# Causal attention: one mask matmul in front of a bank's scores, in place of one behind each score

## The chip, the cores and the metric

The kernel runs on one core of a Trainium2 chip. The metric is the device time of one execution in microseconds; the time before is a median of three runs.

## The reference

Four layers run one after another over x of 8 sequences x 512 rows x 256: causal attention, attention with four experts behind it ("ffn"), attention with relative positions over 256 steps, and the ffn layer again. Only the first is touched:

```python
attn = jnp.einsum('bhqd,bhkd->bhqk', q, k) * scale          # 16 heads of 16
causal = jnp.tril(jnp.ones((t, t), dtype=bool))
attn = jnp.where(causal, attn, -jnp.inf)
attn = _custom_softmax(attn)    # clip to +-100, max, exp, sum + 1e-6, + 1e-8, normalise again
out = jnp.einsum('bhqk,bhkd->bhqd', attn, v)
```

## The kernel before

`attention` walks over sequences n (0 to 7 are the causal layer, 8 to 15 the first ffn layer; both run in one stream). A sequence has 4 groups g of 4 heads, and a group 4 slots kt, one for each block of 128 keys. In a slot the engines run hand-written programs, in step by semaphores.

TensorE makes scores twice. `score` (L474) makes them with queries on partitions, two groups ahead, into a ring of three banks of PSUM, `sc`; VectorE reduces each unit to maxima (`row_max`, L769). `score_t` (L495) makes them with keys on partitions and the maximum already subtracted, into a ring of two banks, `sct`; ScalarE takes exponentials of each unit (`exp`, L690), VectorE clips them (`clip`, L798), and `pv` (L526, L534) multiplies by v. The stacked operands are bf16 in 96 or 99 rows, q and k being split in three parts each.

In the causal layer a unit holds as many heads as fit a bank of 512 columns. For `score` with qt = 0 that is four heads of 128 columns, with qt = 1 two of 256, with qt = 2 and 3 one of 384 or 512. For `score_t` it is the other way round: kt = 3 four heads, kt = 2 two, kt = 1 and 0 one. So each group has 11 units in either direction. Behind each head's score a second matmul adds the mask of the diagonal block, 128 columns: identity times `mask_qk` (L477) or `mask_kq` (L498), which hold 0 or -1e30. Only the last matmul of a unit tells the reader (`sc_ps`, `t_ps`), and a unit's first waits until its bank is free (`max_done`, `exp_done`).

`floor_row` (L509) is a matmul of 3 rows and 512 columns into the `sct` ring, whose exponential gives the lower clip (L697). Between units a slot fits in a "light" use of bank gen1 (transposes L404, L438, L446, L457) and, at its end, half of a "heavy" use of bank gen0 (L413, L421, L430: f32 projections of the neighbouring sequences). A heavy use stands behind the last unit of the slot: at kt = 0 and 1 that is a `score_t` unit, at kt = 2 and 3 a floor row. `heavy_at` names one for slots 0 to 7 and 12 to 15, and for 8 to 11 that of the sequence before. In the first sequence slots 0 to 3 and 8 to 11 have none.

Of the kernel before, what the change touches and what calls it, by code (L numbers as in the profile page):

```python
# [12 lines left out]
P = 128  # L13
NB, T, D = 8, 512, 256
# [35 lines left out]
def attention(nc, M, R, S, C, A, layers, first, end, units):  # L50
# [10 lines left out]
    def causal(n):  # L61
        return layers[n // NB].causal
# [16 lines left out]
    last = end - 1  # L79
# [25 lines left out]
    def score_heads(n, qt, i):  # L105

        if causal(n) and qt == 0:
            return (0, 1, 2, 3) if i == 0 else ()
        if causal(n) and qt == 1:
            return (i, i + 1) if i % 2 == 0 else ()  # L110
        return (i,)

    def max_unit(n, g, qt, i):

        at = (0, 1 + i // 2, 3 + i, 7 + i)[qt] if causal(n) else 4 * qt + i
        return sum(NG * MAX_UNITS[causal(m)] for m in range(n)) + MAX_UNITS[causal(n)] * g + at

    def exp_heads(n, kt, i):

        if causal(n) and kt == 3:  # L120
            return (0, 1, 2, 3) if i == 0 else ()
        if causal(n) and kt == 2:
            return (i, i + 1) if i % 2 == 0 else ()
        return (i,)

    def floors_at(n, g, kt):

        fn, fg = group(n, g + 1)
        if not (exists(fn) and causal(fn)):
            return {}  # L130
        return {i: (fn, fg, h) for i, h in {2: ((1, 0), (3, 1)), 3: ((1, 2), (3, 3))}.get(kt, ())}
# [10 lines left out]
    for n in range(first, end):  # L142
        for g in range(NG):
            for kt in range(KT):
                for i in range(4):
                    if exp_heads(n, kt, i):
                        number((n, g, kt, i))
                    if i in floors_at(n, g, kt):
                        fn, fg, h = floors_at(n, g, kt)[i]
                        number((fn, fg, "floor", h))  # L150

    def exp_unit(n, g, kt, i):
        return unit_no[(n, g, kt, i)]
# [72 lines left out]
    with nc.Block(no_gpsimd_drain=True) as block:  # L226
# [161 lines left out]
        def _(pe):  # L388
# [71 lines left out]
            def score(n, g, qt, i):  # L460

                heads = score_heads(n, qt, i)
                if not heads:
                    return
                if qt == 0 and i == 0:
                    pe.wait_ge(S.stack_loaded[g], 64 * (n + 1))
                u = max_unit(n, g, qt, i)
                if u >= 3:
                    pe.wait_ge(S.max_done, u - 2)
                bank = M.sc[u % 3]  # L470
                cols = P * (qt + 1) if causal(n) else T
                for at, h in enumerate(heads):
                    o = at * cols
                    last = nc.tensor.matmul(bank[:, o:o + cols], M.stack_q[0:96, g, h, qt * P:qt * P + P], M.stack_k[0:96, g, h, 0:cols],  # L474
                                            start=True, stop=True)
                    if causal(n):
                        last = nc.tensor.matmul(bank[:, o + qt * P:o + qt * P + P], C.ident_bf[:, :], C.mask_qk[:, :],  # L477
                                                start=False, stop=True, skip_group_check=True)
                last.then_inc(S.sc_ps, 1)

            def score_t(n, g, kt, i):

                heads = exp_heads(n, kt, i)
                if not heads:
                    return
                if kt == 0 and i == 0 and not causal(n):
                    pe.wait_ge(S.max_rows[g], 16 * (n + 1))
                u = exp_unit(n, g, kt, i)
                if u >= 2:
                    pe.wait_ge(S.exp_done, u - 1)  # L490
                bank = M.sct[u % 2]
                q0 = kt * P if causal(n) else 0
                for at, h in enumerate(heads):
                    o = at * (T - q0)
                    last = nc.tensor.matmul(bank[:, o:o + T - q0], M.stack_k[0:99, g, h, kt * P:kt * P + P], M.stack_q[0:99, g, h, q0:T],  # L495
                                            start=True, stop=True)
                    if causal(n):
                        last = nc.tensor.matmul(bank[:, o:o + P], C.ident_bf[:, :], C.mask_kq[:, :],  # L498
                                                start=False, stop=True, skip_group_check=True)
                last.then_inc(S.t_ps, 1)  # L500

            def floor_row(n, g, i):
# [42 lines left out]
            def slot(n, g, kt):  # L545
                s = KT * g + kt
                tn, tg = group(n, g + 2)
                floors = floors_at(n, g, kt)
                light, heavy = light_at(n, s), heavy_at(n, s)
                for i in range(4):  # L550
                    score_t(n, g, kt, i)
                    if exists(tn):
                        score(tn, tg, kt, i)
                    if i in floors:
                        floor_row(*floors[i])
                    if i == (2 if kt == KT - 1 else 0) and light:
                        use_bank(light)
                    if i == (2 if causal(n) else 1):
                        pv_before(n, g, kt)
                if heavy:  # L560
                    use_bank(heavy, halves=(s % 2,))
# [3 lines left out]
            for qt in range(KT):  # L565
                for i in range(4):
                    score(first, 0, qt, i)
                use_bank(opening[8 + qt])
            for qt in range(KT):
                for i in range(4):  # L570
                    score(first, 1, qt, i)
                if qt < 3:
                    use_bank(opening[12 + qt])
# [2020 lines left out]
```

## Time and profile before

| | |
|---|---|
| median of three runs | 2650.02 us (2644.34 to 2658.11) |
| the profiled execution, device time | 2654.06 us |
| its span, first to last instruction | 2652.3 us |
| instructions | 46652 |
| TensorE's mean granted clock | 0.971 of full |
| TensorE, VectorE, ScalarE, POOL busy | 93%, 69%, 54%, 50% of the span |

An engine's busy time is the union of its instructions. Matmul rows overlap: a row's duration holds the stream of its columns and the tail of the pipeline, so the pitch between starts, not the duration, is what a matmul costs in a row of them. "PEld" is the loading of weights, which can run under the matmul before it.

### The profile page before, as it was taken

How to read it: one execution, taken by the hardware profiler on the slowest of the kernel's cores; microseconds unless marked ns; L12 is line 12 of the kernel's file. 1: busy time of each engine (PE TensorE's matmuls, PEld its weight loads, DVE VectorE, ACT ScalarE, POOL GpSimd, SP SyncE). 2: the span in 40 equal slices, each digit the busy share in tenths (PEclk: the TensorE clock that was granted, in tenths of full speed). 3: DMA queues.
4: the chain of work that ended last, by engine and by line, in shares of the span. 5: the costliest groups of instructions: out<-in, count | busy, mean ns of one | idle time of the engine just before them, and what ended most of it. 6: DMA issues, size and time to landing. Idle time of an engine off the chain costs nothing. (4 is left out here: it accounts for less than half of the span.)

```text
span 2652.3 us, 46652 instructions
## 1 busy us (share of the span) xinstructions
PE 2465.1 (93%) x15144; PEld 1430.2 (54%) x15144; DVE 1835.1 (69%) x3682; ACT 1438.0 (54%) x2991; POOL 1332.1 (50%) x1349
## 2 busy tenths in 40 slices
PE   6999999999999999989996899976999999989998
PEld 3555555554444444368886466652344444349897
DVE  5988999898788887843333457666778888844333
ACT  3666666666777777643332222113777777753332
POOL 5455666553345554246555466644235554445555
PEclk9999999999999999999998799988999999999999
DMA  5333333343434444145554000004434444335554
GB/s 161 94 109 97 109 108 101 106 117 101 121 113 126 126 130 120 53 150 193 195 177 155 22 1 17 17 24 133 120 109 131 129 129 121 94 113 168 195 195 137
DMA packets 249650, 305.92 MB, mean 115 GB/s; under 512 B 27746, under 2 KB 224577, under 8 KB 249412
## 3 DMA queue, kind: packets, MB, share of 16 engines
q1 hardware_dynamic: 237876, 275.37, 34.8%
q0 software_dynamic: 10176, 26.27, 2.8%
q8 instruction: 125, 2.05, 0.3%
q10 hardware_dynamic: 1360, 1.31, 0.2%
q14 instruction: 113, 0.93, 0.1%
HBM read 210.32 MB, written 92.84 MB: 114 GB/s over the span
## 5 line engine op out<-in xcount | busy, mean ns | idle before, releaser
L769 DVE TENSOR_REDUCE neg_max_af<-sc_af 128x1 f32<-128x512 f32 (+3 forms) x864 | 551.1, 663 | 109.5 <-PE sc_af L474 84.5
L690 ACT ACTIVATE prob_af<-sct_af 128x512 f32<-128x512 f32 (+1 forms) x864 | 484.5, 582 | 249.1 <-PE sct_af L495 137.4
L769 DVE TENSOR_REDUCE neg_max_f<-sc_f 128x1 f32<-128x512 f32 x512 | 334.0, 685 | 92.1 <-PE sc_f L474 90.1
L690 ACT ACTIVATE prob_f<-sct_f 128x512 f32<-128x512 f32 x512 | 291.0, 598 | 134.8 <-PE sct_f L495 133.0
L474 PE MATMUL sc_af<-stack_k_af,stack_q_af 96*128 96x512 bf16 (+3 forms) x1024 | 332.2, 345 | 19.3 <-DVE neg_max_af L769 13.4
L495 PE MATMUL sct_af<-stack_q_af,stack_k_af 99*128 99x512 bf16 (+3 forms) x1024 | 331.3, 346 | 5.2 <-ACT prob_af L690 4.4
L1598 PE MATMUL y_ps_e<-w_r,hT_e 128*128 x1120 | 258.5, 384 | 7.5 <-issue 5.6
L798 DVE SCALAR_TENSOR_TENSOR prob_af<-prob_af,w_r 128x512 f32<-128x512 f32 (+2 forms) x224 | 231.5, 1042 | 25.9 <-ACT prob_af L690 25.7
L526 PE MATMUL out_af<-prob_af,v_aug_af 128*32 128x512 f32 (+3 forms) x2048 | 232.3, 525 | 6.8 <-DVE prob_af L798 5.9
L1598 PEld LDWEIGHTS y_ps_e<-w_r,hT_e 128*128 128x128 f32 x1120 | 209.4, 192 | 38.4 <-issue 11.9
L495 PEld LDWEIGHTS sct_af<-stack_q_af,stack_k_af 99*128 99x128 bf16 x1024 | 100.1, 98 | 228.5 <-ACT prob_af L690 147.6
L1783 DVE TENSOR_TENSOR y_e<-y_ps_e,b_e 128x256 f32<-128x256 f32 x70 | 29.7, 425 | 279.4 <-PE y_ps_e L1598 276.7
L1611 PE MATMUL hT_ps_e<-xT_e,w_r 128*128 128x128 f32 x1856 | 219.7, 277 | 3.2 <-DMA w_r<-in_f_W_dram 2.0
L1611 PEld LDWEIGHTS hT_ps_e<-xT_e,w_r 128*128 128x128 f32 x1856 | 218.0, 194 | 7.2 <-DMA w_r<-in_f_W_dram 3.1
L474 PE MATMUL sc_f<-stack_k_f,stack_q_f 96*128 96x512 bf16 x512 | 195.4, 387 | 20.4 <-DVE neg_max_f L769 13.3
L1668 ACT ACTIVATE xT_e<-xT_ps_e 128x256 f32<-128x256 f32 x70 | 26.9, 385 | 332.4 <-PE xT_ps_e L1589 332.4
L495 PE MATMUL sct_f<-stack_q_f,stack_k_f 99*128 99x512 bf16 x512 | 195.3, 384 | 4.5 <-ACT prob_f L690 3.3
L474 PEld LDWEIGHTS sc_af<-stack_k_af,stack_q_af 96*128 96x128 bf16 x1024 | 102.1, 100 | 127.6 <-DVE neg_max_af L769 54.0
L1679 ACT ACTIVATE hT_e<-hT_ps_e,b_r 128x128 f32<-128x128 f32 x560 | 152.8, 383 | 32.1 <-issue 25.7
L1050 POOL TENSOR_TENSOR parts_af<-qkf_af,parts_af 128x512 bf16<-128x512 f32 x62 | 76.6, 1236 | 127.7 <-ACT parts_af L668 127.6
L526 PE MATMUL out_f<-prob_f,v_aug_f 128*32 128x512 f32 x1024 | 137.0, 607 | 0.8 <-ACT prob_f L690 0.7
L495 PEld LDWEIGHTS sct_f<-stack_q_f,stack_k_f 99*128 99x128 bf16 x512 | 49.6, 98 | 159.0 <-ACT prob_f L690 120.1
(373 smaller groups left out, 4744.7 us busy)
## 6 DMA issues: line engine op xcount, KB each, us to landing
w_r<-in_f_W_dram SPq DMA_DIRECT2D x66, 1024.0 KB, 5.0
stack_k_af<-k_parts_d SPq DMA_DIRECT2D x64, 384.0 KB, 4.2
k_parts_d<-parts_af SPq DMA_DIRECT2D x187, 128.0 KB
q_parts_d<-parts_af SPq DMA_DIRECT2D x96, 128.0 KB
stack_q_af<-q_parts_d SPq DMA_DIRECT2D x64, 192.0 KB, 3.0
stack_k_f<-k_parts_d SPq DMA_DIRECT2D x32, 384.0 KB, 4.3
w_next<-in_f_W_dram SPq DMA_DIRECT2D x12, 1024.0 KB, 4.9
k_parts_d<-parts_f SPq DMA_DIRECT2D x91, 128.0 KB
```

Source lines behind the costliest of these rows:

```text
L474: last = nc.tensor.matmul(bank[:, o:o + cols], M.stack_q[0:96, g, h, qt * P:qt * P + P], M.stack_k[0:96, g, h, 0:cols], start=True, stop=True)
L495: last = nc.tensor.matmul(bank[:, o:o + T - q0], M.stack_k[0:99, g, h, kt * P:kt * P + P], M.stack_q[0:99, g, h, q0:T], start=True, stop=True)
L526: last = nc.tensor.matmul(bank[32 * i:32 * i + 32, q0:T], M.v_aug[:, kt, 4 * g + i, :], M.prob[:, kt % 2, i, 0:T - q0], start=(kt == 0), s ...
L690: nc.scalar.activation(dst, src.rearrange("p (h q) -> p h q", h=len(heads)), ACT.Exp).then_inc(S.exp_done, 1)
L769: nc.vector.tensor_reduce(M.neg_max[:, qt, heads[0]:heads[-1] + 1], src, AX.X, ALU.max, negate=True).then_inc(S.max_done, 1)
L798: nc.vector.scalar_tensor_tensor(out=p, in0=p, scalar=1.0, in1=M.floor[:, g % 2, hs, kt * P:T], op0=ALU.min, op1=ALU.max).then_inc(S.clip_ ...
L1050: nc.gpsimd.tensor_tensor(M.parts[:, j, 1, :], full, top, ALU.subtract).then_inc(S.split_step, 1)
L1598: last = nc.tensor.matmul(y_ps[:, 0:D], hT[s % 2][:, c, :], w2[:, c, e, :], start=(c == 0), stop=(c == FC - 1))
L1611: last = nc.tensor.matmul(hT_ps[2 * (s % 2) + f][:, q * P:q * P + P], w1[n % NW][:, c, cols], xT[:, c, :], start=(c == 0), stop=(c == DC - 1))
L1668: nc.scalar.activation(xT[:, :, :], xT_ps[:, 0:D].rearrange("p (c t) -> p c t", c=DC), ACT.Copy).then_inc(xT_ready, 1)
L1679: last = nc.scalar.activation(hT[s % 2][:, 4 * f + q, :], hT_ps[2 * (s % 2) + f][:, q * P:q * P + P], ACT.Relu, bias=b1[:, e, 4 * f + q:4 ...
L1783: nc.vector.tensor_tensor(y[i][:, :], y_ps[:, 0:D], b2[:, e, :], ALU.add).then_inc(y_ready, 1)
```

## The change

In the causal layer `score` and `score_t` now begin a unit with one matmul that writes the masks of all heads of the bank: the output is a view of heads x 128 columns, the moving operand is the mask repeated with a step of 0, and it starts the bank. The scores follow without a start, so they add where the mask has written and overwrite elsewhere. The unit's last matmul, which tells the reader, is now a score. Layers that aren't causal get the instructions they had.

```diff
--- before.py
+++ after.py
@@ -469,13 +469,15 @@
                     pe.wait_ge(S.max_done, u - 2)
                 bank = M.sc[u % 3]
                 cols = P * (qt + 1) if causal(n) else T
+                masked = causal(n)
+                if masked:
+                    diagonal = bank[:, 0:len(heads) * cols].rearrange("p (h k) -> p h k", h=len(heads))[:, :, qt * P:qt * P + P]
+                    nc.tensor.matmul(diagonal, C.ident_bf[:, :], C.mask_qk[:, :].unsqueeze(1).to_broadcast([P, len(heads), P]),
+                                     start=True, stop=True)
                 for at, h in enumerate(heads):
                     o = at * cols
                     last = nc.tensor.matmul(bank[:, o:o + cols], M.stack_q[0:96, g, h, qt * P:qt * P + P], M.stack_k[0:96, g, h, 0:cols],
-                                            start=True, stop=True)
-                    if causal(n):
-                        last = nc.tensor.matmul(bank[:, o + qt * P:o + qt * P + P], C.ident_bf[:, :], C.mask_qk[:, :],
-                                                start=False, stop=True, skip_group_check=True)
+                                            start=not masked, stop=True, skip_group_check=masked)
                 last.then_inc(S.sc_ps, 1)
 
             def score_t(n, g, kt, i):
@@ -490,13 +492,15 @@
                     pe.wait_ge(S.exp_done, u - 1)
                 bank = M.sct[u % 2]
                 q0 = kt * P if causal(n) else 0
+                masked = causal(n)
+                if masked:
+                    diagonal = bank[:, 0:len(heads) * (T - q0)].rearrange("p (h q) -> p h q", h=len(heads))[:, :, 0:P]
+                    nc.tensor.matmul(diagonal, C.ident_bf[:, :], C.mask_kq[:, :].unsqueeze(1).to_broadcast([P, len(heads), P]),
+                                     start=True, stop=True)
                 for at, h in enumerate(heads):
                     o = at * (T - q0)
                     last = nc.tensor.matmul(bank[:, o:o + T - q0], M.stack_k[0:99, g, h, kt * P:kt * P + P], M.stack_q[0:99, g, h, q0:T],
-                                            start=True, stop=True)
-                    if causal(n):
-                        last = nc.tensor.matmul(bank[:, o:o + P], C.ident_bf[:, :], C.mask_kq[:, :],
-                                                start=False, stop=True, skip_group_check=True)
+                                            start=not masked, stop=True, skip_group_check=masked)
                 last.then_inc(S.t_ps, 1)
 
             def floor_row(n, g, i):
```

The first place is on TensorE, in the slot s = 4 of a sequence (kt = 0), where a score unit of four heads stands between two score_t units of one head. In the changed kernel L475 and L498 are the masks, L479 and L502 the scores.

```order
+L475 MATMUL sc_af<-mask_qk,ident_bf 128x512
+L479 MATMUL sc_af<-stack_k_af,stack_q_af 128x128 x4
 L404 MATMUL gen_af<-ident,w_2_r 128x128 x4
-L495 MATMUL sct_af<-stack_q_af,stack_k_af 128x512
-L498 MATMUL sct_af<-mask_kq,ident_bf 128x128
-L495 MATMUL sct_af<-stack_q_af,stack_k_af 128x512
-L498 MATMUL sct_af<-mask_kq,ident_bf 128x128
```

The four masks of 128 columns have become one of 512 ahead of four scores; the pairs of score and mask that the removed rows show are turned round (below).

The second place is the end of that slot on TensorE: the last score_t unit, the heavy use L430, and the first units of the next slot.

```order
+L498 MATMUL sct_af<-mask_kq,ident_bf 128x128
+L502 MATMUL sct_af<-stack_q_af,stack_k_af 128x512
 L430 MATMUL gen_af<-wa_o,attT_af 128x256 x2
-L495 MATMUL sct_af<-stack_q_af,stack_k_af 128x384
-L498 MATMUL sct_af<-mask_kq,ident_bf 128x128
-L474 MATMUL sc_af<-stack_k_af,stack_q_af 128x256
-L477 MATMUL sc_af<-mask_qk,ident_bf 128x128
-L474 MATMUL sc_af<-stack_k_af,stack_q_af 128x256
-L477 MATMUL sc_af<-mask_qk,ident_bf 128x128
+L498 MATMUL sct_af<-mask_kq,ident_bf 128x128
+L502 MATMUL sct_af<-stack_q_af,stack_k_af 128x384
+L475 MATMUL sc_af<-mask_qk,ident_bf 128x2x128
```

L430 stood behind a mask of 128 columns and now stands behind a score of 512; the two-head unit's masks have become one of 2 x 128 columns. The other engines' programs keep their instructions and their order.

## Rows read from the trace of the kernel before

**Rows 1.** The page, busy us of each engine, share, instructions
```profile
PE 2465.1 (93%) x15144; PEld 1430.2 (54%) x15144; DVE 1835.1 (69%) x3682; ACT 1438.0 (54%) x2991; POOL 1332.1 (50%) x1349
```

**Rows 2.** Windows: length, busy us of PE, PEld, DVE, ACT, POOL, then granted clock
```profile
60.00:120.00 60.00, 57.65 (x498) 29.95 (x498) 54.65 (x106) 40.77 (x77) 20.92 (x22) 0.94 0.39 106
120.00:600.00 480.00, 468.31 (x3987) 254.67 (x3987) 438.26 (x827) 317.75 (x588) 284.78 (x255) 0.98 0.37 105
600.00:620.00 20.00, 18.94 (x146) 9.29 (x144) 19.76 (x37) 11.52 (x21) 2.07 (x3) 1.00 0.24 68
```

**Rows 3.** Waits from 120 to 600 us: us in total, times, longest
```profile
ACT prob_af L690 <- PE sct_af L498: 90.4, 134, 1.8
...
PEld sc_af L474 <- DVE neg_max_af L769: 28.6, 49, 0.8
...
PEld sct_af L495 <- ACT prob_af L690: 24.6, 52, 0.8
DVE prob_af L798 <- ACT prob_af L690: 23.4, 42, 1.4
...
DVE neg_max_af L769 <- PE sc_af L477: 7.2, 22, 0.4
...
DVE neg_max_af L769 <- PE sc_af L474: 1.2, 1, 1.2
```

**Rows 4.** Timeline, a score_t unit of four heads: start, us, engine, line
```profile
300.58 0.22 PE L495 MATMUL sct_af<-stack_q_af,stack_k_af 99*128 99x128 bf16 x1
...
300.99 0.22 PE L498 MATMUL sct_af<-mask_kq,ident_bf 128*128 128x128 bf16 x1
```

**Rows 5.** Timeline, a score unit of one head, and the next
```profile
301.05 0.38 PE L474 MATMUL sc_af<-stack_k_af,stack_q_af 96*128 96x512 bf16 x1
...
301.27 0.22 PE L477 MATMUL sc_af<-mask_qk,ident_bf 128*128 128x128 bf16 x1
```

**Rows 6.** Timeline, a score unit of two heads
```profile
310.05 0.27 PE L474 MATMUL sc_af<-stack_k_af,stack_q_af 96*128 96x256 bf16 x1
...
310.16 0.22 PE L477 MATMUL sc_af<-mask_qk,ident_bf 128*128 128x128 bf16 x1
...
310.22 0.27 PE L474 MATMUL sc_af<-stack_k_af,stack_q_af 96*128 96x256 bf16 x1
```

**Rows 7.** Timeline, a score_t unit behind a wait
```profile
73.49 0.10 PEld L495 LDWEIGHTS sct_af<-stack_q_af,stack_k_af 99*128 99x128 bf16 x1 [0.23 <-issue]
73.50 0.23 PE L495 MATMUL sct_af<-stack_q_af,stack_k_af 99*128 99x128 bf16 x1
...
73.56 0.22 PE L498 MATMUL sct_af<-mask_kq,ident_bf 128*128 128x128 bf16 x1
```

**Rows 8.** Timeline, a mask with f32 weights behind it
```profile
308.85 0.22 PE L498 MATMUL sct_af<-mask_kq,ident_bf 128*128 128x128 bf16 x1
308.85 0.30 PEld L430 LDWEIGHTS gen_af<-wa_o,attT_af 128*128 128x128 f32 x2
308.91 0.43 PE L430 MATMUL gen_af<-wa_o,attT_af 128*128 128x256 f32 x1
```

**Rows 9.** Line L430 from 120 to 600 us: ns min/median/max
```profile
L430 PE MATMUL gen_af<-wa_o,attT_af x104: 377/379/483, 166.0 to 597.9; 128*128 128x256 f32 x104
```

**Rows 10.** Timeline, four f32 matmuls of 256 columns
```profile
308.91 1.08 PE L430 MATMUL gen_af<-wa_o,attT_af 128*128 128x256 f32 x4
```

**Rows 11.** Windows of TensorE's clock at its lower level, and of two lulls
```profile
138.90:142.30 3.40, 2.40 (x18) 0.59 (x15) 3.40 (x7) 1.08 (x2) 3.15 (x4) 1.00 0.54 191
142.40:145.70 3.30, 3.30 (x14) 1.81 (x15) 2.72 (x9) 1.52 (x3) 0.00 (x0) 0.50 0.46 114
...
569.10:572.40 3.30, 3.30 (x15) 1.86 (x14) 2.88 (x9) 1.65 (x3) 0.00 (x0) 0.50 0.47 112
352.00:357.00 5.00, 4.00 (x29) 1.68 (x28) 4.90 (x12) 1.76 (x4) 4.39 (x4) 1.00 0.54 192
```

## The prediction

> **What bounds the kernel now.** I began with the page's busy shares [rows 1]: TensorE is busy for 93% of the span, VectorE for 69%. A busy matmul row holds its pipeline's tail too, so 93% doesn't yet say that TensorE is the bound. The windows by stage [rows 2] come next. The causal layer's steady part is the stretch from 60 to 620 us, at 0.98 of TensorE's full clock in its middle; almost nothing that the diff touches runs elsewhere. In its middle 480 us TensorE shows 468.3 us and VectorE 438.3 us, ScalarE 317.8 and POOL 284.8: two engines are near their limit. The waits of that stretch [rows 3] say who is late for whom. VectorE waits 23.4 us for exponentials of ScalarE and 7.2 + 1.2 us for scores: 31.8 us in 480. ScalarE waits for a score_t unit that ends in a mask 90.4 us (134 times). TensorE's weight loads wait 28.6 us for a maximum to free a score bank and 24.6 us for an exponential to free a score_t bank. So it is a ring of three engines: TensorE fills a bank, ScalarE or VectorE empties it, and VectorE, with 438.3 busy and 31.8 waiting, is nearest to being the bound. A microsecond saved on TensorE is worth at most a microsecond, and nothing where a bank was the late thing.
>
> **What the change removes.** Each group of four heads has, in either direction, one unit of four heads (128 columns each), two units of two heads (256 each) and eight units of one head. There are 8 sequences x 4 groups x 2 directions = 64 such sets. Before, a set holds 16 mask matmuls of 128 columns = 2048 columns; after, one of 512, two of 256 and eight of 128 = 2048 columns. **No column is saved**; 5 matmuls and 5 weight loads per set are, 320 of each.
>
> What one is worth is read from its pitch. In the four-head unit eight matmuls of 128 columns start from 300.58 to 300.99 [rows 4]: 0.41 / 7 = 0.058 us each, loads included, so loads are hidden. The durations 0.22 and 0.38 for 128 and 512 columns [rows 4, 5] give 0.16 / 384 = 0.417 ns a column, 53 ns per 128, so about 5 ns of each matmul is fixed. A two-head unit goes 0.11, 0.06 [rows 6] and agrees. Saved: 320 x 5 ns = **1.6 us** of TensorE. The Trainium skill, "TensorE: Matmul & The Clock Gate", section "Wait — 56ns, not 53.3ns?", gives 2.5 ns as the fixed part; by it the sum would have 0.8 us here. The trace's pitch is the longer one.
>
> **What the change moves.** The mask goes from the end of a unit to its front. Four consequences.
>
> (a) The wait for a bank now stands ahead of the mask's weight load, not ahead of the score's. Queued behind it are the same matmuls, so nobody waits longer. Would a short first matmul expose the next load? At 73.49 a unit starts behind such a wait with a 128-column matmul at 73.50, and the next starts at 73.56 [rows 7]: 0.06, the usual pitch. The bounds are nothing, and one exposed stream of 0.05 us at each of the 101 loads that ended a wait in the middle 480 us (49 + 52), 5 us there and 6 in the stage. I take 0, since the row is the very case.
>
> (b) The last matmul of a unit, which releases ScalarE or VectorE, is now the score. For one head its end is the same sum: 0.22 + 0.06 before, 0.06 + 0.22 after. Cost 0.
>
> (c) A score now adds to the mask's columns, and the distance between two writes of one column stays 128 columns or more, as from 301.05 to 301.27 before [rows 5], where the mask followed without a gap. Cost 0.
>
> (d) What follows a unit follows a long matmul, not one of 58 ns. That matters for f32 weights. At 308.85 the mask starts and with it the load of L430's f32 weights; the matmul starts at 308.91 and takes 0.43 [rows 8], while the median of L430 is 379 ns [rows 9]. So 0.43 - 0.38 = 0.05 us of the load is exposed. After the change a score of 384 or 512 columns (at least 0.16 us) covers it. This place (a "heavy" bank use right behind the last score_t unit, with no wait that drains the queue between) comes at slots with kt 0 or 1, 8 per sequence, less 4 in the first: 60 x 0.05 = **3.0 us**. At kt 2 and 3 a floor row of 512 columns stands between already, and nothing changes.
>
> Sum: 1.6 + 3.0 = 4.6 us of TensorE's time, 0.17% of the run. VectorE, ScalarE, POOL and both DMA queues issue what they did, in their order. How much arrives? If TensorE were the bound everywhere, 4.6; if VectorE were, none. With VectorE waiting 31.8 us in the ring and TensorE's loads 53.2 us for banks, I take somewhat under half: **2 us**. The profiled execution took 2654.06 us (span 2652.3), 4.0 above the median of the three runs, 2650.02; so I expect about 2652.1 for a like execution and **2648.0** for the median.
>
> **A cost the trace doesn't show.** The masks of two heads are written as two runs of 128 columns with a gap of 128, and the moving mask is read again and again by a step of 0. No matmul of before writes such a pattern. The Trainium skill, "PSUM — Partial Sum Buffer", section "Specifications (TRN2)", says that any non-contiguous access pattern slows matmuls significantly, which speaks against this change. From rows: the lower end is no cost, a bf16 row of 256 columns at 0.11 [rows 6]. The upper end is what f32 takes for as many columns: four matmuls of 256 fill 1.08 us, the last one's 0.38 among it, so the pitch is 0.70 / 3 = 0.23 [rows 9, 10], and 0.46 for 512. That is 128 x (0.23 - 0.11) + 64 x (0.46 - 0.22) = 15.4 + 15.4 = 31 us. I take 0, because each run is 128 columns long and the nearest row is that of the same type.
>
> **The rivals.**
> 1. *Nothing arrives.* VectorE's 438.3 of 480 us sets the pace and the 4.6 us become longer waits of weight loads. Time 2650.0.
> 2. *Slower: the pattern.* The strided or repeated mask runs slower. The saving is eaten when the 192 wide masks take over 4.6 / 192 = 24 ns more each; at the upper end 31 - 4.6 = 26.4 us are lost and the time is 2676. Against it: each run is long. At half of the upper end 2661.
> 3. *Faster: the clock.* TensorE's clock stood at its lower level, 1.2 GHz (granted 0.50), in five stretches of some 3.3 us between 120 and 600 us (the first and the last stand in [rows 11]), the first after a lull at 138.9 to 142.3, where TensorE was busy 2.40 of 3.40 us; near 352 us a similar lull (4.00 of 5.00) had none. Each costs half its length, 1.7 us. If the shift removes all five and all of the 4.6 us arrives: 8.5 + 4.6 = 13.1, time 2637. The same thing can add the missing ones, +3 us or so.
> 4. *The change doesn't do what it says.* If scores beside the diagonal added to a bank's old values, results would change, but no engine's row would: all counts of instructions are fixed. Time as forecast.
>
> **How the numbers follow.** The forecast has a chance of 0.58, rival 1 0.22, rival 2 0.08, rival 3 0.10, rival 4 0.02. A measurement of this kernel can tell about 0.5%, 13.3 us, from no change: under 2636.8 or over 2663.3. Rival 3, whose end lies at the line, gives 0.06 beyond it and 0.04 within; rival 2 gives 0.06 beyond and 0.02 within. So 0.06 faster, 0.88 the same, 0.06 slower. The range: low end, all 4.6 us and three clock stretches gone, 2650 - 4.6 - 5.1 = 2640; high end, no gain, two stretches more and a quarter of the pattern's upper price less the saving (7.7 - 4.6 = 3.1), 2650 + 3.4 + 3.1 = 2656.5, taken as 2657.
>
> **What would show it.** In the profile after, masks on TensorE number 704, in forms of 128, 256 and 512 columns. A four-head unit starts its scores 0.22 us behind the mask and a two-head one 0.11; 0.4 or more there means rival 2. L430 behind a score takes 379 ns, not 0.43 us. ScalarE's wait for the last matmul of a score_t unit and VectorE's 31.8 us fall by a few us together. If instead the loads' waits for banks (53.2 us) grow by what was saved, rival 1 is right. The prediction is wrong if the time leaves 2640 to 2657 with clock and pitches as before.

## The result and the profile after

The changed kernel takes **2639.38 us** (median of five, 2636.45 to 2640.8) against 2650.5 us, the median of the kernel before with two more runs; the ratio is 0.9953 (95% interval 0.9933 to 0.9974). Timed again beside other kernels (12 runs) it took 2639.61 us, ratio 0.9957 (0.9940 to 0.9974). So 11 us came where 2 were forecast, and the time lies 0.6 us under the range's low end of 2640.

The page of the kernel after, its busy times [rows 1 before]:

```profile
span 2637.6 us, 46012 instructions
...
PE 2443.5 (93%) x14824; PEld 1406.5 (53%) x14824; DVE 1837.7 (70%) x3682; ACT 1437.0 (54%) x2991; POOL 1334.0 (51%) x1349
```

TensorE lost exactly 320 matmuls and 320 loads. VectorE, ScalarE and POOL have their counts and, within 3 us, their busy time. The windows of the causal layer [rows 2]:

```profile
60.00:120.00 60.00, 57.61 (x463) 28.74 (x463) 54.94 (x107) 40.47 (x77) 20.59 (x22) 0.94 0.40 111
120.00:600.00 480.00, 465.65 (x3784) 244.68 (x3785) 446.31 (x844) 322.32 (x596) 287.95 (x257) 1.00 0.37 106
```

In the same 480 us VectorE does 446.3 us of work, not 438.3, and TensorE's clock is at 1.00, not 0.98. The waits of that stretch [rows 3]:

```profile
ACT prob_af L694 <- PE sct_af L502: 84.2, 132, 1.9
...
PEld sc_af L475 <- DVE neg_max_af L773: 33.4, 60, 0.8
...
PEld sct_af L498 <- ACT prob_af L694: 25.8, 56, 0.8
...
DVE prob_af L802 <- ACT prob_af L694: 18.4, 38, 1.4
...
DVE neg_max_af L773 <- PE sc_af L479: 5.4, 14, 1.2
```

VectorE waits 18.4 + 5.4 = 23.8 us, not 31.8, ScalarE 84.2, not 90.4, and the loads wait 33.4 + 25.8 = 59.2 us for banks, not 53.2. The PE timeline of a four-head unit with its neighbours, and of L430 behind a score [rows 4, 8]:

```profile
299.06 0.38 PE L502 MATMUL sct_af<-stack_q_af,stack_k_af 99*128 99x512 bf16 x1
299.28 0.38 PE L475 MATMUL sc_af<-mask_qk,ident_bf 128*128 128x512 bf16 x1
299.50 0.39 PE L479 MATMUL sc_af<-stack_k_af,stack_q_af 96*128 96x128 bf16 x4
```

```profile
305.13 0.27 PE L475 MATMUL sc_af<-mask_qk,ident_bf 128*128 128x256 bf16 x1
305.24 0.38 PE L479 MATMUL sc_af<-stack_k_af,stack_q_af 96*128 96x256 bf16 x2
...
306.78 1.03 PE L430 MATMUL gen_af<-wa_o,attT_af 128*128 128x256 f32 x4
```

The mask of four heads takes 0.22 us to the first score, the strided one of two heads 0.11. Four scores of 128 columns fill 0.39 us: (0.39 - 0.22) / 3 = 0.057 or a little less each. L430's four take 1.03 us, not 1.08 [rows 10]: the exposed 0.05 us is gone.

L413, another f32 projection, stood behind a mask in the slots kt 0 and 1 as well. Its ns (min, median, max) before and after, from 60 to 620 us; the median falls by 54 ns:

```profile
L413 PE MATMUL gen_af<-xnT_af,wa_qkv x96: 592/646/1183, 111.4 to 498.3; 128*128 128x512 f32 x96
```

```profile
L413 PE MATMUL gen_af<-xnT_af,wa_qkv x96: 590/592/1222, 110.4 to 491.3; 128*128 128x512 f32 x96
```

**Where the time went.** Two words first. TensorE's stream is what its instructions need one behind the other, by their pitches. A fall is a stretch of some 3.4 us in which TensorE's granted clock is 0.50, that is 1.2 GHz; a sequence without one is called undisturbed. The last read of a sequence's output (ScalarE, `o_sb`, L676 before, L680 after) marks the pace. Before:

```profile
128.61 0.64 ACT L676 ACTIVATE o_sb_af<-out_af 128x512 f32<-128x512 f32 x1
200.09 0.64 ACT L676 ACTIVATE o_sb_af<-out_af 128x512 f32<-128x512 f32 x1
343.03 0.64 ACT L676 ACTIVATE o_sb_af<-out_af 128x512 f32<-128x512 f32 x1
413.35 0.64 ACT L676 ACTIVATE o_sb_af<-out_af 128x512 f32<-128x512 f32 x1
555.11 0.64 ACT L676 ACTIVATE o_sb_af<-out_af 128x512 f32<-128x512 f32 x1
```

After:

```profile
127.44 0.64 ACT L680 ACTIVATE o_sb_af<-out_af 128x512 f32<-128x512 f32 x1
197.16 0.64 ACT L680 ACTIVATE o_sb_af<-out_af 128x512 f32<-128x512 f32 x1
336.59 0.64 ACT L680 ACTIVATE o_sb_af<-out_af 128x512 f32<-128x512 f32 x1
407.49 0.64 ACT L680 ACTIVATE o_sb_af<-out_af 128x512 f32<-128x512 f32 x1
546.92 0.64 ACT L680 ACTIVATE o_sb_af<-out_af 128x512 f32<-128x512 f32 x1
```

In each fence the first two rows are one sequence apart, the next two another, and from the first to the last are six. Before, a sequence takes 71.48 us (first pair) where TensorE's clock fell in it and 70.32 (second pair) or 70.28 (the next) where it did not: a fall costs about 1.2 us. After, it takes 69.72 without and 70.90 with. Six take 426.5 us before and 419.5 after. An undisturbed sequence is thus 70.28 - 69.71 = 0.57 us shorter, 8 x 0.57 = 4.6 us in the layer: **the whole saving of the stream**. The other part is falls. Before, they stand in four of the six sequences, three of them in a row. Windows of the kernel before [rows 11], and the one fall in the six after:

```profile
142.50:145.70 3.20, 3.20 (x14) 1.71 (x14) 2.62 (x8) 1.42 (x3) 0.00 (x0) 0.50 0.47 114
214.20:217.40 3.20, 3.20 (x16) 1.92 (x15) 2.81 (x9) 1.53 (x3) 0.00 (x0) 0.50 0.54 113
285.80:289.00 3.20, 3.20 (x17) 2.16 (x16) 3.02 (x10) 1.40 (x3) 0.00 (x0) 0.50 0.21 70
```

```profile
350.10:353.30 3.20, 3.20 (x8) 1.20 (x8) 2.91 (x9) 1.02 (x2) 0.00 (x0) 0.50 0.44 121
```

The falls before stand 71.7 us apart, and a sequence with a fall in it is 71.5 us long. That near match became the theory of the pace, below. The whole of the layer ends 11 us earlier (the `o_sb` of the eighth sequence ends at 631.1 before, 620.1 after).

### The profile page after: what moved, and what is told of

Its sections match the earlier page's. It is cut to its first block and busy times, and to the rows that moved or that the text cites. A ratio compares the mean times of both kernels' runs of the same rounds, so it can differ in the third digit from the quotient of the medians.

```text
span 2637.6 us, 46012 instructions
## 1 busy us (share of the span) xinstructions
PE 2443.5 (93%) x14824; PEld 1406.5 (53%) x14824; DVE 1837.7 (70%) x3682; ACT 1437.0 (54%) x2991; POOL 1334.0 (51%) x1349
## 5 line engine op out<-in xcount | busy, mean ns | idle before, releaser
L479 PE MATMUL sc_af<-stack_k_af,stack_q_af 96*128 96x512 bf16 (+3 forms) x1024 | 319.7, 342 | 11.1 <-DVE neg_max_af L773 10.9
L502 PE MATMUL sct_af<-stack_q_af,stack_k_af 99*128 99x512 bf16 (+3 forms) x1024 | 319.7, 343 | 5.1 <-ACT prob_af L694 3.9
L479 PE MATMUL sc_f<-stack_k_f,stack_q_f 96*128 96x512 bf16 x512 | 195.7, 388 | 21.6 <-DVE neg_max_f L773 14.3
L502 PE MATMUL sct_f<-stack_q_f,stack_k_f 99*128 99x512 bf16 x512 | 195.6, 384 | 5.5 <-ACT prob_f L694 3.9
L502 PEld LDWEIGHTS sct_af<-stack_q_af,stack_k_af 99*128 99x128 bf16 x1024 | 97.5, 98 | 193.0 <-ACT prob_af L694 115.9
L1683 ACT ACTIVATE hT_e<-hT_ps_e,b_r 128x128 f32<-128x128 f32 x560 | 152.4, 382 | 32.5 <-issue 25.8
L479 PEld LDWEIGHTS sc_af<-stack_k_af,stack_q_af 96*128 96x128 bf16 x1024 | 98.8, 99 | 81.5 <-DVE neg_max_af L773 21.9
L502 PEld LDWEIGHTS sct_f<-stack_q_f,stack_k_f 99*128 99x128 bf16 x512 | 49.7, 98 | 160.0 <-ACT prob_f L694 119.7
```

Of the source, the lines that this page charges most:

```text
L1683: last = nc.scalar.activation(hT[s % 2][:, 4 * f + q, :], hT_ps[2 * (s % 2) + f][:, q * P:q * P + P], ACT.Relu, bias=b1[:, e, 4 * f + q:4 ...
```

## The experiments

Each kernel was timed beside the kernel before on the same chip, and profiled. The table reads three things from each profile by the `o_sb` rows and the granted clock: an undisturbed sequence, the falls of the clock in six sequences, and the time of the six. The kernel before and the changed one have several profiles; their falls and times stand in order (after, after_again, after_third, after_side). Not all kernels were timed on the same chip, so they are best compared by their ratios.

| kernel | median us | ratio (interval) | undisturbed, us | falls | six, us |
|---|---|---|---|---|---|
| before | 2648.6 to 2652.8 | 1 | 70.28 | 4, 4, 3 | 426.5, 426.5, 425.3 |
| after | 2639.4, 2639.6 | 0.9953, 0.9957 | 69.71 | 1, 2, 2, 1 | 419.5, 420.7, 422.6, 419.5 |
| order_only | 2640.28 | 0.9966 (0.9946 to 0.9986) | 69.89 | 0 | 419.4 |
| merge_only | 2641.63 | 0.9974 (0.9957 to 0.9991) | 70.07 | 1 | 421.6 |
| heavy_front | 2640.59 | 0.9970 (0.9955 to 0.9986) | 69.97 | 1 | 421.0 |
| after_mask_twice | 2653.32 | 1.0016 (0.9998 to 1.0035) | 71.45 | 0 | 428.8 |
| twice_score_t | 2652.18 | 1.0009 (0.9989 to 1.0028) | 70.88 | 2 | 428.4 |
| twice_score | 2649.05 | 0.9993 (0.9974 to 1.0012) | 71.17 | 1 | 428.3 |
| before_lull_filled | 2655.07 | 1.0012 (0.9994 to 1.0031) | 70.28 | 2 | 424.5 |
| after_lull_filled | 2648.17 | 0.9995 (0.9979 to 1.0011) | 69.72 | 2 | 422.6 |
| after_paced | 2644.54 | 0.9985 (0.9963 to 1.0007) | 70.01 | 0 | 420.1 |
| before_slowed | 2654.49 | 1.0017 (0.9997 to 1.0037) | 70.93 | 2 | 428.6 |
| after_at_70 | 2649.55 | 1.0011 (0.9990 to 1.0033) | 70.32 | 3 | 428.1 |
| floor_first | 2633.85, 2630.61 | 0.9945, 0.9926 (0.9906 to 0.9946) | 69.15 | 3, 3 | 415.4, 415.3 |

### The parts of the change alone

**order_only**: every mask in front of its own score, none merged; `score` gets the same edit.

```diff
+                    front = causal(n)
+                    if front:
+                        nc.tensor.matmul(bank[:, o:o + P], C.ident_bf[:, :], C.mask_kq[:, :],
+                                         start=True, stop=True)
                     last = nc.tensor.matmul(bank[:, o:o + T - q0], ...
-                                            start=True, stop=True)
-                    if causal(n):
+                                            start=not front, stop=True, skip_group_check=front)
+                    if causal(n) and not front:
...
```

> Every head's mask stands in front of its own score, none is merged: 1024 masks of 128 columns as before. Stream theory (what TensorE's stream is shortened by arrives in full; the exposed f32 loads go, 3.0 us, the 320 matmuls stay): 2650.5 - 3 = 2647.5, an undisturbed sequence of the causal layer 70.3 - 0.4 = 69.9 us. Rival, the buffers set the pace and the gain of the change came from the falls of TensorE's clock alone: sequences stay at 70.3 us, and the time follows how many falls of the clock stand in the stage (six before, one after, each worth 1.2 us of the sequence it falls in).

**merge_only**: the changed kernel, but one-head units keep the mask behind.

```diff
-                masked = causal(n)
+                masked = causal(n) and len(heads) > 1
...
+                    if causal(n) and not masked:
+                        last = nc.tensor.matmul(bank[:, o:o + P], C.ident_bf[:, :], C.mask_kq[:, :], ...
```

> Units of two and four heads get the one mask in front, units of one head keep theirs behind the score. Stream theory: the 320 matmuls go (1.6 us), the exposed f32 loads behind one-head units stay: 2649, sequence 70.1 us. If instead the merge carries the gain, the time is that of the change, near 2639 to 2641, sequence 69.7 us.

**heavy_front**: the first edit in `score_t` alone, for the units ahead of a heavy use.

```diff
-                    front = causal(n)
+                    front = causal(n) and kt < 2 and i == 3
```

> Only the last score_t unit of the slots with kt 0 and 1 has its mask in front, 64 units, 60 of them with a heavy bank use behind. Stream theory: the first matmul of L413, L421 and L430 there loses its 0.05 us, 60 x 0.05 = 3.0 us, all of it arrives, 2647.5, the same as order_only. If the order matters elsewhere too (at every unit), order_only is faster than this by more than 1 us a stage and this one stays near 2650.

Undisturbed sequences went from 70.28 to 69.89, 70.07 and 69.97: 0.39, 0.21 and 0.31 us, times eight 3.1, 1.7 and 2.5 us, where 3.0, 1.6 and 3.0 were expected. The first two add up to 0.60, near the whole change's 0.57. **The stream theory holds to a tenth of a microsecond a sequence, and so does the split.** Most of the gain of the order (0.31 of 0.39) lies in 64 units of 704. But all three kernels are 7 to 9 us faster by their ratios, some 5 us more than their stream, and all three profiles have no fall or one where the kernel before has three or four. A cause beside the stream was needed.

### Is all of TensorE's stream the bound?

**after_mask_twice** issues the mask of each one-head unit twice; **twice_score_t** and **twice_score** do so in one direction.

```diff
                     nc.tensor.matmul(diagonal, C.ident_bf[:, :], C.mask_kq[:, :]...
+                    if len(heads) == 1:
+                        nc.tensor.matmul(diagonal, C.ident_bf[:, :], C.mask_kq[:, :]...
```

> The changed kernel with the mask of each one-head unit issued twice: 512 more matmuls of 0.058 us, 29.7 us of TensorE's stream, 3.7 a sequence. Stream theory: all of it arrives, 2639.4 + 29.7 = 2669, an undisturbed sequence 69.7 + 3.7 = 73.4 us. If VectorE or the buffers set the pace and TensorE has room: under half, 2639 to 2654, a sequence under 71.5 us.

> The changed kernel with the mask of the one-head score_t units (slots kt 0 and 1) issued twice: 256 x 0.058 = 14.8 us of TensorE's stream, 1.86 a sequence. Doubling both directions cost 1.76 of 3.71 us a sequence. Theory of places: in the slots kt 0 and 1 TensorE is the bound and all of it arrives, undisturbed sequence 69.7 + 1.8 = 71.5 us, time 2639 + 14 = 2653. Rival, the same half everywhere: 70.6 us, 2646.

> The same for the one-head score units (slots kt 2 and 3), 14.8 us of stream too. Theory of places: these slots wait for VectorE's maxima, TensorE has room, and nothing or little arrives: sequence 69.7 to 69.9 us, 2640. Rival, half everywhere: 70.6 us, 2646.

The sequence grew by 1.74 us for 3.71 us of stream; in score_t alone by 1.17 of 1.86, in score alone by 1.46 of 1.86. So the theory of places is wrong (in the slots kt 2 and 3, where little or nothing was to arrive, 1.46 us did), and so is half everywhere: each half costs well over half by itself, both together under half. Additions find room that the removals did not need; how that room is shared between the slots stays open. The waits of after_mask_twice from 120 to 600 us show VectorE drawn in:

```profile
DVE prob_af L808 <- ACT prob_af L700: 21.2, 45, 1.4
DVE neg_max_af L779 <- PE sc_af L482: 17.9, 53, 1.2
```

VectorE waits 39.1 us, against 23.8 after the change.

### The falls of the clock

**before_lull_filled** and **after_lull_filled** issue the two floor rows of slot 3 twice.

```diff
+                if fill:
+                    nc.tensor.matmul(M.sct[u % 2][:, :], M.stack_k[96:99, g, i, 0:P], M.stack_q[96:99, g, i, :],
+                                     start=True, stop=True)
...
-                        floor_row(*floors[i])
+                        floor_row(*floors[i], fill=s == 3)
```

> The kernel before, with the two floor rows of slot 3 of each causal sequence issued twice (16 more matmuls of 512 columns, 3.5 us of TensorE's stream), where TensorE stood idle for VectorE and the clock fell just behind. Clock theory: the falls of slot 3 go, each was worth 1.2 us, and the added stream lies in the lull: 2650 - 5 to 2650 - 6, about 2644, with undisturbed sequences of 70.3 us. Rival (falls are chance): no fewer falls, and the time is 2650 or up to 3.5 us more.

> The same filling in the changed kernel, which had one such fall. Clock theory: no gain, 2639 to 2642; sequences 69.7 us if the lull hides the filling, up to 70.1 if it doesn't. Rival: the same as before_lull_filled less 11 us.

> The kernel before, profiled once more. If the falls of TensorE's clock in the causal layer belong to the kernel (a sequence of 71.5 us with a fall in it, 71.7 us from fall to fall), this profile has 4 or more of them between 130 and 620 us again. If they are chance, it has 0 to 2, as the profiles of the variants had, and the six sequences take 422 us in place of 426.5.

> The changed kernel, profiled once more: 0 to 1 falls between 130 and 620 us if they belong to the kernel, any number to 5 if they are chance. The undisturbed sequence is 69.7 us either way.

The second profiles speak against chance in the kernel before, which has four falls again, at 141.7, 213.4, 425.0 and 496.7 (and a fifth at 568.4). For the changed kernel the expectation was missed: from 130 to 620 us it has three falls (349.5, 421.2, 561.1) where 0 to 1 were expected, two of them in the six sequences. The filling of the kernel before is half a miss. Its profile has undisturbed sequences of 70.28, so the lull hid the added stream, and two falls, not four. Yet the timed median is 2655, not 2644, and the filled changed kernel's 2648.17 is some 9 us over the changed kernel's. The filling does not simply remove falls, and why its timed runs were slower than its profiled stage is not explained here.

**after_paced** and **before_slowed** change the length of a sequence by doubled masks in slots kt 0 and 1, ten a sequence in the changed kernel and twenty in the old one.

```diff
+                    if kt == 0 and i in (1, 2) or kt == 1 and i == 1 and g in (0, 2):
+                        nc.tensor.matmul(diagonal, C.ident_bf[:, :], C.mask_kq[:, :]...
```

```diff
+                        for _ in range(2 if kt == 0 or kt == 1 and i == 1 else 1):
                             last = nc.tensor.matmul(bank[:, o:o + P], C.ident_bf[:, :], C.mask_kq[:, :], ...
```

> The changed kernel with ten masks a sequence issued twice in slots kt 0 and 1 (0.58 us), so that an undisturbed sequence is 70.3 us again, as before the change. Theory of the pace: TensorE's clock fell four times in six sequences before because a sequence with a fall in it, 71.5 us, is as long as the distance from fall to fall, 71.7, so one fall brings the next; here 3 to 5 falls again and 2649. Rival, the falls hung on what stood in the lull: 0 to 2 falls and only the added stream, 2639.4 + 4.6 = 2644.

> The kernel before with twenty masks a sequence issued twice in slots kt 0 and 1, 1.17 us of stream, 9.3 us in all, so that an undisturbed sequence is 71.4 us, as it was with a fall. Theory of the pace: a fall now makes a sequence of 72.6, which no longer meets the next fall, 0 to 1 falls in six sequences, and the time rises by 9.3 - 5 = 4 to 2654. Rival: four falls stay, 2650 + 9 = 2659.

Both missed their lengths, since about half of an addition arrives: 70.01 in place of 70.3, and 70.93 in place of 71.4. At 70.01 there was no fall and the time was the rival's, 2644.54. Its profile ends the layer as early as the changed kernel's do (621.9 us, against 621.2 in the mean), so the 5 us between the medians are not explained. At 70.93 there were two falls, between the theory's 0 to 1 and the rival's four, and the time rose by 4 us as the theory had it, though 5.2 us of stream arrived. Neither kernel had the length that it was made for, so neither tells the theories apart. **after_at_70** doubles the masks that before_slowed did, in the changed kernel.

```diff
+                    if kt == 0 or kt == 1 and i == 1:
+                        nc.tensor.matmul(diagonal, C.ident_bf[:, :], C.mask_kq[:, :]...
```

> The changed kernel with the mask of five score_t units a group issued twice (20 a sequence, 1.17 us of stream; half of such additions arrived so far), so that an undisturbed sequence is 70.3 us, as before the change. Theory of the pace: 3 to 5 falls of the clock in six sequences again, time 2649. Rival, the falls belong to the old order of instructions: 0 to 2 falls, time 2639.4 + 5 = 2644.

> The kernel before, third profile. Falls that belong to the kernel: 3 to 5 in six sequences, 425 to 427.5 us. Chance: 0 to 2.

> The changed kernel, third profile: 0 to 2 falls in six sequences and 418.3 to 420.7 us if the low count belongs to it, 3 or more if it is chance.

It has the new order and the old length. Its `o_sb` rows and windows:

```profile
127.97 0.59 ACT L683 ACTIVATE o_sb_af<-out_af 128x512 f32<-128x512 f32 x1
198.29 0.59 ACT L683 ACTIVATE o_sb_af<-out_af 128x512 f32<-128x512 f32 x1
```

```profile
211.70:214.90 3.20, 3.20 (x7) 1.17 (x7) 3.03 (x10) 0.73 (x2) 0.13 (x1) 0.50 0.40 121
283.40:286.60 3.20, 3.20 (x7) 1.17 (x7) 3.03 (x10) 0.73 (x2) 0.12 (x1) 0.50 0.36 108
355.10:358.30 3.20, 3.20 (x7) 1.17 (x7) 3.03 (x10) 0.73 (x2) 0.12 (x1) 0.50 0.41 123
358.30:361.50 3.20, 3.20 (x23) 2.19 (x25) 1.29 (x4) 2.03 (x4) 0.00 (x0) 0.50 0.67 160
426.80:430.00 3.20, 2.70 (x16) 0.86 (x17) 3.20 (x6) 0.82 (x2) 2.04 (x3) 1.00 0.47 163
```

A sequence is 70.32 us, three falls stand in a row 71.7 us apart, as in the kernel before (its third profile has 212.6, 284.3 and 356.0), and the time is 2649.55 us. The third of them is twice as long as the others, as its two windows show. The median is 10 us over the changed kernel's (15 by the ratios), where 8 x 0.61 = 4.9 us of stream arrived, and the layer ends at 630.7 us in the profile, where it ended at 630.0 before the change and at 621.2 after it in the mean. The execution profiled took 2641.37 us all the same, at the low end of its kernel's: the layers behind were short in it.

All profiles together say more than this one. In the five whose undisturbed sequence is 70.28 to 70.33 us (the kernel before three times, before_lull_filled, after_at_70), 12 of the 16 falls in the six sequences were followed by another 71.7 us later. In those of another length, floor_first aside, it was 1 of 15. before_lull_filled fits in: its falls at 423.8 and 495.5 are a chain with a third at 567.2. In all of these kernels the falls in the six sequences begin 13.3 to 14.2 us behind the start of the `o_sb` row ahead of them.

**The falls go with the length of the sequence rather than with the order of the masks**: a fall comes at nearly the same place in a sequence, it stretches the sequence to 71.5 or 71.7 us, and that is nearly the distance at which the next fall then came. At 69.7 to 70.1 us the chain breaks after one or two. What begins a chain, and why some kernels have a single fall and others none, stays open. The third profile of the changed kernel has its two falls, as expected, but takes 422.6 us for the six, over the 420.7 expected, because one of the two is of double length. Its windows:

```profile
349.30:352.50 3.20, 3.20 (x6) 1.06 (x6) 3.01 (x10) 0.85 (x2) 0.10 (x1) 0.50 0.25 71
352.60:355.80 3.20, 3.20 (x29) 2.30 (x31) 1.62 (x3) 2.14 (x5) 0.00 (x0) 0.50 0.79 199
```

### The same mechanism where the change didn't reach

**floor_first**: in slots kt 2 and 3 the floor row of i = 3 goes ahead of the score unit, so that a heavy use follows a score, with no wait between.

```diff
                     score_t(n, g, kt, i)
+                    if i in floors and i == 3:
+                        floor_row(*floors[i])
                     if exists(tn):
                         score(tn, tg, kt, i)
-                    if i in floors:
+                    if i in floors and i != 3:
                         floor_row(*floors[i])
```

> The changed kernel with the floor row of i = 3 (slots kt 2 and 3) ahead of the score unit, not behind it, so that the heavy f32 matmuls there follow a score with no wait between: their first matmul falls from 697 to 592 ns (L413) or from 483 to 379 (L421, L430), 60 x 0.105 = 6.3 us of stream. Theory that a saving ahead of the projections arrives in full: 2639.4 - 6.3 = 2633, an undisturbed sequence 69.7 - 0.8 = 68.9. Rival, the score unit now waits behind the floor row's bank and VectorE gets its scores later: 69.7 or more, 2640 to 2645.

> The changed kernel beside floor_first. If the gain of the change is 4.6 us of stream and some 5 us of falls of the clock: 8 to 11 us under the kernel before. If the falls were luck of the first occasion, 4 to 6 us under.

> 0.55 us a sequence less than the changed kernel in its profile (69.15 against 69.7), 4.4 us in all: 4 to 6 us under after_side. Rival, the falls of the clock it had (three) take it back: 0 to 2 us under.

Beside the changed kernel on one chip it took 2630.61 us against 2639.61, 9 us less, and 0.9926 (0.9906 to 0.9946) of the kernel before: **it beats both**. The first time, on another chip, it took 2633.85 us, as expected, but its ratio was 0.9945, only just under the changed kernel's 0.9953 and 0.9957, so how much it gains on that one is less sure than that it does. Its `o_sb` rows in the second profile:

```profile
125.66 0.64 ACT L682 ACTIVATE o_sb_af<-out_af 128x512 f32<-128x512 f32 x1
194.81 0.64 ACT L682 ACTIVATE o_sb_af<-out_af 128x512 f32<-128x512 f32 x1
...
540.92 0.64 ACT L682 ACTIVATE o_sb_af<-out_af 128x512 f32<-128x512 f32 x1
```

L430 in the changed kernel, where 14 of its first matmuls follow a floor row and take 483 ns, and in floor_first (second profile), from 60 to 620 us:

```profile
L430 PE MATMUL gen_af<-wa_o,attT_af x112: 377/379/483, 163.4 to 597.8; 128*128 128x256 f32 x112
```

```profile
L430 PE MATMUL gen_af<-wa_o,attT_af x112: 377/378/382, 161.8 to 591.9; 128*128 128x256 f32 x112
```

The matmuls of 483 ns, 0.10 us longer than the median, are gone. A sequence is 69.15 us, 0.56 less where 0.8 was expected, and six take 415.3. It has three falls; two of them were followed by another after 68.3 us. They begin 12.4 to 13.9 us behind the `o_sb` row, near the place of the others, but each stretches its sequence by 0.15 us only; why so little stays open. 4.5 of the 9 us are stream; the expectation of 4 to 6 missed the rest.

## Why the prediction was wrong

**What was right.** The sizes in the stream: 1.6 us for the 320 matmuls (merge_only showed 1.7), 3.0 us for the f32 loads (order_only 3.1, heavy_front 2.5). The three terms put at nothing have little room to be more: order_only, which holds all three, saved 3.1 us where the f32 term alone is 3.0. Behind a wait the score follows its mask at the usual pitch, 306.55 and 306.62 in the changed kernel:

```profile
306.55 0.23 PE L498 MATMUL sct_af<-mask_kq,ident_bf 128*128 128x128 bf16 x1
306.62 0.33 PE L502 MATMUL sct_af<-stack_q_af,stack_k_af 99*128 99x384 bf16 x1
```

The unknown price was nothing too: the strided mask of two heads has a pitch of 0.11 us and the repeated one of four 0.22, those of plain rows. The Trainium skill, "PSUM — Partial Sum Buffer", says in "Specifications (TRN2)" that any non-contiguous pattern slows matmuls significantly; with runs of 128 columns the trace doesn't agree. Rival 2 fell.

**The step that failed** is "How much arrives?". I took 2 of 4.6 us because VectorE seemed nearest to the bound. All 4.6 arrived: 70.28 to 69.71 us a sequence. VectorE's 31.8 us of waits were the mark of TensorE's stream, and 8 of them went. Here a busy share of 91% in the second engine (438.3 of 480) was no sign that it takes a saving back. The sign I had named for rival 1 failed too: the loads' waits for banks did grow, by 6.0 us, beside the fall of the other engines' waits that I had named for the forecast. Both signs came at once, while the sequence got shorter, so the loads' waits can't tell the two apart. The "half" I expected holds for additions, which the runs put at 47 to 78%, not for this removal.

**The second error** was to treat the clock as luck that could only widen the range. Rival 3 named the mechanism and gave it 0.10, all or nothing. It was mostly systematic: the old length of a sequence invites a chain of falls (4, 4 and 3 in three profiles), the new one doesn't (1, 2, 2, 1). In the mean over the profiles of each kernel the six sequences take 5.5 us less (426.1 and 420.6): 3.4 of stream, and 2.1 for 2.2 falls fewer. With the opening and the eighth sequence, which hold the layer's other falls, it is 8.8 us by the end of the layer (630.0 and 621.2), 4.6 of it stream; the other 4.2 I put down to falls, though those outside the six weren't priced one by one. The last 2 us of the 11 lie in layers the change doesn't touch, where profiles of one kernel differ by 8 to 11 us; they are not explained. I had priced a fall at half its length, 1.7 us; most cost 1.2. The low end of the range, the stream and three falls at 1.7 us, is 2640; with falls at 1.2 it would have been 2642. That the time missed the range by no more than 0.6 us is thus partly luck: the low end stood on too high a price.

The forecast that the change would stay within 0.5% stood: it is 0.43 to 0.47%. But that it could hardly be told from no change did not, as both intervals lie below 1.

## What to carry to other kernels

Read the pace of a repeated unit of work, with and without a disturbance, rather than the busy shares: 0.6 us in 70.3 was plain there, and it gave every part of the change its price. Look at what stands ahead of a matmul with f32 weights: a short matmul, or a wait, leaves part of the load exposed (here 0.05 us behind the mask and 0.10 behind a floor row that waits), and moving a long matmul there without a wait gained both times, in the change and in floor_first. And where a loop's length is near the distance between two falls of TensorE's clock, a small saving can be worth double, and a small addition too, as one of each was here.

## What was not expected of the hardware

The same 3.4 us at 1.2 GHz did not cost the same everywhere: about 1.2 us a sequence in the kernels before and after, 1.4 to 1.5 in before_lull_filled, after_at_70 and before_slowed, and 0.15 in floor_first. Falls twice as long, 6.8 us, one each in after_lull_filled, after_third and after_at_70, cost 2.9, 3.2 and 3.4. And matmuls of 128 columns of one kind in a row start 55 ns apart where masks between them made it 58, so a merge saved a little more in the four-head unit than the fixed parts of its three masks.
